# Four layers of attention and convolution on one core: scores of one image beside the output of the other, item 0 by chunks, out blocks in banks 6 and 7, and another filling of the last item

## What is computed

```
x = x + L0(_gn(x))   # lambda layer: q, k, v, softmax over positions, relative table
x = x + L1(_gn(x))   # 16 heads of 64, causal: 8 look back, 8 ahead; output projection Wo
x = x + L2(_gn(x))   # 16 heads of 64, attention with relative positions per head
x = x + L3(_gn(x))   # 3x3 convolution, tensor-train channel product, bias, relu
```

## Time and profile before

| | us |
|---|---|
| median of 3 runs (1408.1 to 1410.59) | 1408.25 |
| profiled execution, its own time | 1407.82 |
| its span | 1406.0 |
| PE busy (96% of the span) | 1348.8 |
| POOL busy (45%) | 627.2 |
| DVE busy (43%) | 608.4 |
| ACT busy (31%) | 436.7 |
| granted TensorE clock, mean | 0.987 |

### The profile page before, as it was taken

The page is one execution under the profiler, slowest core; times in us unless marked ns, Lnnn a source line. Parts: engine busy times, 40 slices in busy tenths (PEclk is TensorE's granted clock), DMA queues, the critical chain, the costliest instruction groups (busy, mean ns, idle before and its releaser), DMA issues.

```text
span 1406.0 us, 20610 instructions
## 1 busy us (share of the span) xinstructions
PE 1348.8 (96%) x7792; PEld 1057.7 (75%) x7792; DVE 608.4 (43%) x1385; ACT 436.7 (31%) x1053; POOL 627.2 (45%) x715
## 2 busy tenths in 40 slices
PE   4899889799999999999999999999999999999998
PEld 3688755457777787777788788788877887877887
DVE  6423422683454324445332445444144654356222
ACT  2220112022434311344330244534114444333222
POOL 2332279025454565545447443443654644445000
PEclk9999989999999999999999999999999999999999
DMA  5111035012222233222223221121322221210011
GB/s 192 38 46 45 30 61 92 0 40 71 67 74 69 68 84 85 72 68 68 69 68 98 67 62 53 61 66 56 85 81 60 61 61 54 68 54 23 1 54 66
DMA packets 57122, 89.23 MB, mean 63 GB/s; under 512 B 6880, under 2 KB 19840, under 8 KB 57024
## 3 DMA queue, kind: packets, MB, share of 16 engines
q1 hardware_dynamic: 55024, 84.59, 21.1%
q10 hardware_dynamic: 2000, 3.32, 0.7%
HBM read 79.50 MB, written 4.19 MB: 60 GB/s over the span
## 4 chain that ended last, share of the span: by engine, by line
PE 83%; DVE 2%; ACT 1%; issue 0%; POOL 0%; ACTq 0%; DVEq 0%; POOLq 0%
PE PS L1016 51%; PE PS L1493 6%; PE PS L1072 4%; PE PS L1090 3%; PE PS L856 3%; PE PS L1104 2%; PE PS L1060 2%; PE PS L862 2%; PE PS L1114 2%; PE PS L1133 2%; PE PS L1510 2%; DVE part L840 1%; PE PS L874 1%; PE PS L1081 1%; PE PS L1065 1%
## 5 line engine op out<-in xcount | busy, mean ns | idle before, releaser
L1016 PE MATMUL PS<-XB,w_hi 128*128 128x512 f32 x1024 | 359.4, 408 | 3.4 <-DVE XB L390 3.4
L210 POOL CAST w_hi<-w_raw 128x512 fp32r<-128x512 f32 x195 | 122.2, 627 | 402.5 <-PE PS L1016 294.3
L212 POOL TENSOR_TENSOR w_lo<-w_raw,w_hi 128x512 fp32r<-128x512 f32 x195 | 256.2, 1314 | 15.6
L1016 PEld LDWEIGHTS PS<-XB,w_hi 128*128 128x128 f32 x1024 | 192.7, 188 | 53.0 <-issue 7.2
L1016 PE MATMUL PS<-XB,w_lo 128*128 128x512 f32 x512 | 202.4, 395 | 0.0
L1016 PE MATMUL PS<-XB,part 128*128 128x512 f32 x768 | 200.2, 405 | 0.0
L1213 ACT ACTIVATE part<-PS,nmax 128x256 f32<-128x256 f32 (+1 forms) x256 | 111.5, 459 | 170.7 <-DVE nmax L1306 106.9
L1016 PEld LDWEIGHTS PS<-XB,part 128*128 128x128 f32 x768 | 140.8, 189 | 31.4
L210 POOL CAST part<-part 128x512 fp32r<-128x512 f32 x85 | 52.6, 619 | 150.9 <-PE PS L1016 150.9
L212 POOL TENSOR_TENSOR part<-part,part 128x512 fp32r<-128x512 f32 x85 | 110.7, 1302 | 6.8
L1016 PE MATMUL PS<-part,w_hi 128*128 128x512 f32 x344 | 112.2, 393 | 1.1 <-DVE part L1359 1.1
(11 more groups left out here) (142 smaller groups left out, 2033.6 us busy)
## 6 DMA issues: line engine op xcount, KB each, us to landing
w_raw<-in_w SPq DMA_DIRECT2D x187, 256.0 KB, 2.6
part<-in_w SPq DMA_DIRECT2D x85, 256.0 KB, 2.6
part<-part SPq DMA_DIRECT2D x32, 128.0 KB, 4.3
out_x<-xT SPq DMA_DIRECT2D x16, 256.0 KB, 2.1
xT<-in_x ACTq DMA_DIRECT2D x8, 256.0 KB, 8.2
xT<-in_x SPq DMA_DIRECT2D x8, 256.0 KB, 10.9
w_raw<-in_w SPq DMA_DIRECT2D x16, 128.0 KB, 3.8
part<-in_emb ACTq DMA_DIRECT2D x1, 961.0 KB, 13.0
```

The lines of the kernel that those rows point to most:

```text
L210: pool.tensor_copy(hi, raw).then_inc(w_hi_done, 1)
L212: pool.tensor_tensor(lo, raw, hi.bitcast(F32), ALU.subtract).then_inc(w_ready, 1)
L1016: m = nc.tensor.matmul(PS[:, bank, :], wt[:, (c % 4) * P:(c % 4) * P + P], rhs(hl, c), start=c == k == 0, stop=c == CK - 1 and k == 2)
```

## The change

Six edits. **Order on PE in an item**: `attend(i - 1, 1)` moves from the end of item i - 1 to just ahead of `scores(i, 0)`, and `scores(i, 1)` stands just behind `attend(i, 0)`; K and V are cut at other chunks. At a stage's end, attend of image 1 stays in its item, between chunks 3 and 4 of the next V. ACT and DVE follow: `evac_o` and `rest_of_o` move into the next item, `evac_t(i, 0)` ahead of `evac_q`, `evac_k` ahead of `evac_t(i, 1)`. **Out blocks** of stages 0 to 2 go to banks 6 and 7, and the wait for the sums moves from scores to `turn_values` and `attend(i, 0)`. **Item 0**: Q, K and V take turns by chunk over chunks 0 to 3, with V in bank 4, and the half-blocks are loaded in that order. **The last item**: chunks 4 to 7 of V of item 31 stand behind its scores 0, and out blocks 0 and 1 are cut more finely. **Factor products** stand in out blocks 2 to 7 alone, two in the middle and one at the end, where before there were two in each of eight. **Names**: `first_slot[key]` becomes `slots[key, half]`.

```
-        take_item(0)
+        take_item(0, (0,))
+        take_item(0, (1,))
...
+    def bank_of(i, kind):
+        return PT if (i, kind) == (0, "V") else PJ[kind]
     def out_bank(s, o):
-        return (0 if s == 3 else S) + o % 2
+        return (0 if s == 3 else O) + o % 2
...
         def scores(i, a):
-                if i % PAIRS == 0 and i:
-                    pe.wait_ge(sum_done, CK * (i // PAIRS))
         def turn_values(i):
             pe.wait_ge(v_evac, i + 1)
+            if i % PAIRS == 0 and i:
+                pe.wait_ge(sum_done, CK * (i // PAIRS))
         def attend(i, a):
+                if i % PAIRS == 0 and i:
+                    pe.wait_ge(sum_done, CK * (i // PAIRS))
         def out_block(s, o, chunks):
+                if c == 0 and o == 1 and s in (1, 2):
+                    pe.wait_ge(relh_evac, PAIRS * (s - 1) + 1)
+                    pe.wait_ge(relw_evac, PAIRS * (s - 1) + 1)
...
-        for kind in "QKV":
-            project(0, kind, range(CK))
-        for i in range(ITEMS):
-            final = i == ITEMS - 1
-            scores(i, 0)
-            project(i + 1, "Q", range(0, 4))
-            turn_values(i)
-            project(i + 1, "Q", range(4, CK))
-            scores(i, 1)
-            turn_probs(i, 0)
-            project(i + 1, "K", range(0, 2))
-            attend(i, 0)
-            relative(i + 1)
-            project(i + 1, "K", range(2, 6))
-            turn_probs(i, 1)
-            project(i + 1, "K", range(6, CK))
-            attend(i, 1)
-            project(i + 1, "V", range(CK))
...
+        for c in range(4):
+            for kind in "QKV":
+                project(0, kind, range(c, c + 1))
+        for kind in "QKV":
+            project(0, kind, range(4, CK))
+        for i in range(ITEMS - 1):
+            stage_ends = i % PAIRS == PAIRS - 1
+            if i % PAIRS:
+                attend(i - 1, 1)
+            scores(i, 0)
+            project(i + 1, "Q", range(0, 4))
+            turn_values(i)
+            project(i + 1, "Q", range(4, CK))
+            turn_probs(i, 0)
+            project(i + 1, "K", range(0, 3))
+            attend(i, 0)
+            scores(i, 1)
+            relative(i + 1)
+            project(i + 1, "K", range(3, CK))
+            project(i + 1, "V", range(0, 2))
+            turn_probs(i, 1)
+            if stage_ends:
+                project(i + 1, "V", range(2, 4))
+                attend(i, 1)
+                project(i + 1, "V", range(4, CK))
+                for o in range(CK):
+                    out_block(i // PAIRS, o, range(CK))
+            else:
+                project(i + 1, "V", range(2, 4 if i == ITEMS - 2 else CK))
+        i = ITEMS - 1
+        attend(i - 1, 1)
+        scores(i, 0)
+        project(i, "V", range(4, CK))
+        scores(i, 1)
+        out_block(3, 0, range(0, 3))
+        turn_values(i)
+        turn_probs(i, 0)
+        out_block(3, 0, range(3, 6))
+        attend(i, 0)
+        out_block(3, 0, range(6, 7))
+        out_block(3, 1, range(0, 2))
+        turn_probs(i, 1)
+        out_block(3, 1, range(2, 4))
+        attend(i, 1)
+        out_block(3, 1, range(4, 7))
+        for o in range(2):
+            out_block(3, o, range(7, CK))
+        for o in range(2, CK):
+            out_block(3, o, range(0, 4))
+            for k in range(2):
+                build_m(3 * (o - 2) + k)
+            out_block(3, o, range(4, CK))
+            build_m(3 * (o - 2) + 2)
...
     def attention_act(act):
             evac_v(i)
+            if i % PAIRS:
+                evac_o(i - 1)
             exps(i, 0)
+            evac_t(i, 0)
             evac_q(i + 1)
-            evac_t(i, 0)
             exps(i, 1)
             evac_relative(i + 1)
+            evac_k(i + 1)
             evac_t(i, 1)
-            evac_k(i + 1)
-            evac_o(i)
+            if i % PAIRS == PAIRS - 1:
+                evac_o(i)
...
     def attention_dve(dve):
             maxima(i, 0)
+            if j:
+                rest_of_o(i - 1)
             normalize(i, 0)
...
-            rest_of_o(i)
+            if j == PAIRS - 1:
+                rest_of_o(i)
```

More of the change, by code:

```diff
@@ L159, in build, with take, take_item @@
         sources = [None] * CK + list(range(CK, HB0))
[L160 to L166, removed]
+        slots = {}
+        def take(key, layer, kind, number, halves=range(2)):
+            for half in halves:
+                slots[key, half] = len(sources)
+                sources.append(block_at[layer, kind, number, half])
+        def take_item(i, halves=range(2)):
             for kind in "QKV":
-                take((i, kind), STAGES[i // PAIRS][0], kind, i % PAIRS)
-        take_item(0)
+                take((i, kind), STAGES[i // PAIRS][0], kind, i % PAIRS, halves)
+        take_item(0, (0,))
+        take_item(0, (1,))
         for i in range(ITEMS):
@@ L683, in later_layers @@
     w_load, w_split, w_slot, w_wait_used = (g[x] for x in ("w_load", "w_split", "w_slot", "w_wait_used"))
-    w_used, w_ready, slot_of, first_slot = (g[x] for x in ("w_used", "w_ready", "slot_of", "first_slot"))
+    w_used, w_ready, slot_of, slots = (g[x] for x in ("w_used", "w_ready", "slot_of", "slots"))
     w_raw, w_hi, sources = (g[x] for x in ("w_raw", "w_hi", "sources"))
@@ L1000, in later_layers, with chunk_of @@
     LO_KEYS = 2 * PAIRS
+    def bank_of(i, kind):
+        return PT if (i, kind) == (0, "V") else PJ[kind]
     def out_bank(s, o):
-        return (0 if s == 3 else S) + o % 2
+        return (0 if s == 3 else O) + o % 2
     def product_done(eng, key):
-        w_wait_used(eng, first_slot[key] + 1)
+        w_wait_used(eng, slots[key, 1])
     def attention_pe(pe):
-        def chunk_of(n, c, rhs, bank):
-            n += c // 4
+        def chunk_of(key, c, rhs, bank):
+            n = slots[key, c // 4]
             _, hi, lo = w_slot(n)
@@ L1201, in evac_v @@
             if layer_of(i) == 1:
-                ins = nc.scalar.activation(vT, PS[:, PJ["V"], :], ACT.Copy)
+                ins = nc.scalar.activation(vT, PS[:, bank_of(i, "V"), :], ACT.Copy)
             else:
@@ L1400, in attention_dve @@
                 for o in range(CK):
-                    if s == 3:
-                        rest_of_m(dve, 2 * o)
+                    if s == 3 and o >= 2:
+                        rest_of_m(dve, 3 * (o - 2))
+                        rest_of_m(dve, 3 * (o - 2) + 1)
                     add_out(s, o)
@@ L1405, in attention_dve @@
                         stats_of(s, o - 1)
-                    if s == 3:
-                        rest_of_m(dve, 2 * o + 1)
+                    if s == 3 and o >= 2:
+                        rest_of_m(dve, 3 * (o - 2) + 2)
                 stats_of(s, CK - 1)
@@ L1413, in attention_sp @@
             w_load(sp, n)
-            if n == first_slot[1, "Q"]:
+            if n == slots[(1, "Q"), 0]:
                 product_done(sp, (0, "Q"))
@@ L1436, in attention_pool @@
             for k in (2, 3):
-                if n == first_slot[3, "O", 0] + 4 * k:
+                if n == slots[(3, "O", 0), 0] + 4 * k:
                     masked_factor(pool, k)
@@ L1463, in rest_of_m @@
     def rest_of_m(dve, i):
+        if i >= 16:
+            return
         dve.wait_ge(m_hi, i + 1)
```

35 lines of the change are left out of this document (11 added, 24 removed).

## The result

The change made the kernel **slower**: 1415.49 us (median of 6 runs, 1414.26 to 1417.31) against 1408.37 us for the kernel before beside it, a ratio of 1.0054, 95% interval 1.0043 to 1.0065. The prediction said 1399.8 us and gave slower a chance of 0.05.

What follows compares the result with a forecast made beforehand. PE was taken as the bound, busy 1348.8 of 1406.0 us. Terms -3.0 - 4.6 - 4.7 + 4.35 - 0.6 = -8.5 us took 1407.8 to 1399.3, and 0.4 for the median gave 1399.8 us; range 1393.5 to 1405.0.

Steps and rivals of the forecast that it cites:

- Do the ordinary items get a new wait?: Ordinary items of layers 1 and 2: no new wait, 0 us; tightest are layer 1's second probability transposes, slack 1.0 us.
- rival D: Layer 1's 16 items: second probability transposes wait, making the kernel slower; example 1.0 us each, 1415.8 us; chance 0.06.
- Stage starts: At the three stage starts, the 1.0 us waits of scores for the last out-block sum go: -3.0 us.
- Item 0: Projections of item 0: chunk waits go, a 0.8 us weight-split wait comes, scores begin earlier: -4.6 us, bounds -3 to -5.5.
- Rival E: Item 0: the changed order gives nothing beyond half, since weight slots, not chunks, set its pace; 1402 us; chance 0.07.
- Switches in layer 1: Attend directly ahead of scores saves 2.9 us over 14 cross-item pairs, 1.8 over 16 inside items: -4.7 us.
- Rival B: Layer 1: no saving, attend into scores costs what both ways cost before; 1404.5 us; chance 0.11.
- Switches in layer 2: Scores between attend 0 and the relative products add 0.29 us in each of 15 items: +4.35 us, bounds 0 and +6.
- Rival A: Layer 2: scores between attend and the relative products cost nothing; 1395.4 us; chance 0.18.
- Last item: Item 31 to layer 3: old waits and lost clock go, new waits and one clock loss come: -0.6 us, bounds -3 and +3.
- three forecast waits: Item 31: scores 1 for exponentials 3.3 us, block 2 for a weight slot 1.5; layer 3 for the last sum 1.0.
- Rival C: Last item: worse, with the clock at 1.2 GHz for longer behind the 3.3 us wait; +3 us, 1403 us; chance 0.10.

Runs made afterwards that it cites:

- experiment 5: Kernel before with only out blocks of stages 0 to 2 in banks 6 and 7 and the sums' waits behind scores 0: 1404.07 us, ratio 0.9976.
- experiment 4: Kernel before with only the item 0 edit (Q, K, V by chunk over chunks 0 to 3, V in bank 4, half-blocks in that order): 1402.48 us, ratio 0.9963.
- experiment 6: Kernel before with only the new order of PE, ACT and DVE in layer 1's items 0 to 15: 1404.02 us, ratio 0.9973.
- experiment 1: Changed kernel, but in layer 2 ACT's copy of q waits for the relative products of the item before, not both scores: 1400.76 us, ratio 0.9953.
- experiment 2: Changed kernel, but in layer 2 scores 1 stand ahead of the first probability transposes, as before: 1396.50 us, ratio 0.9925.
- experiment 7: Kernel before, but in layer 2 scores 1 stand behind attend 0 and ACT copies transposed probabilities ahead of q: 1424.55 us, ratio 1.0123.

## Why the prediction was wrong

**The step that failed** is the paragraph "Do the ordinary items get a new wait?", which took 0 us. It went through probability transposes, V, the values' transposes, keys, attend and weight splits. Of the relative products it said only "Layer 2 has the relative products besides", as cover for others. But they read q too, and had got a new neighbour without being moved. The step ahead had put scores 1 directly before them and priced three switches there, 0.29 us, without asking what the relative products wait for. The wait is not in the order that PE's rows show; it is in `evac_q`, where ACT waits for both scores of the item. It cost 16 x 0.84 = 13.4 us by the list of waits, some 14.7 us by the stretches (16 x 0.92). The last sentence of the prediction named the sign ("Any wait that repeats per item would make me wrong"), but rival D had it in layer 1, at the probability transposes, and priced the chance of any such wait by that one place. Its example, 1.0 us of wait in each of 16 items and 1415.8 us, comes within 0.4 us of the measured time by coincidence: in layer 1 the probability transposes have no wait at all.

**Stage starts**: -3.0 forecast, -3.5 measured (experiment 5). **Item 0**: -4.6 forecast, -4.1 measured (experiment 4); the split's wait was 1.0 and not 0.8 us, and the 72 products took 17.5 instead of 17.2. Rival E fell. **Switches in layer 1**: -4.7 forecast, -4.8 measured without item 15's wait (experiment 6); an item of 22.7 us. Rival B fell. Scores directly behind attend start 0.84 us after it (338.72 to 339.56), as a 512-column product does (360.06 to 360.90 before); what is paid once less is the 0.11 us of the first product behind attend and the 0.10 us of the way from a product into scores. How the 4.8 us divide between the pairs across items and those inside one was not taken apart:

```profile
338.72 0.91 PE L1122 MATMUL PS<-part,part 128*64 128x128 f32 x16
339.56 0.95 PE L1064 MATMUL PS<-part,part 64*128 64x128 f32 x12
```

The Trainium skill, TensorEngine Tiling (Array Packing), Key Properties, says that changing the tiling mode drains TensorE. Attend (128*64) and scores (64*128) are of two modes by the shapes in these rows, and the trace shows no extra time between them: the scores take 1.09 us behind attend, and 1.09 or 1.12 behind a product of V or Q before. So the page's rule does not give the price here; the rows do.

**Switches in layer 2**: +4.35 forecast, 4.4 to 4.5 measured (experiments 1 and 2), and none once scores 1 stand elsewhere (experiment 2). Rival A fell. **Last item**: -0.6 forecast, +0.6 measured with layer 3, the terms that were mis-sized. All three forecast waits came out within 0.2 us, and the clock stayed at full speed behind layer 3's wait, as forecast. Two gains were counted whole that were worth half. The 1.7 us of lost clock in the old last item were worth 0.85 only (last section): where the clock was not lowered, PE reached its wait earlier and stood longer. And of the 1.5 us of clock won in layer 3, 0.7 went into a new wait: the chain shows PE's products of that stretch released by DVE's chunk, which PE now reaches before it is normalised:

```profile
1318.84 0.61 DVE XB L1612
1319.45 0.04 issue
1319.50 5.58 PE PS L1534 x23
```

-0.6 + 0.85 + 0.7 is +0.95, within 0.4 of what was measured; that rest is open. Nor is +0.6 itself a firm number, as it sets one execution beside one. In the five executions with the old end (before and experiments 4 to 7) last item and layer 3 take 178.8 to 180.6 us together, 179.7 on average, and the profile of before is the longest of them. In the three with the changed end (the changed kernel, experiments 1 and 2) they take 181.2 on average without the 12 products of V. By these the term is +1.5. Rival C had the right sign, but not its reason: the clock behind the new wait lost 1.7 us, about the 1.5 in the sum, and not more.

So the sum of the terms it had was right to about 2 us: with the one wait taken away (experiment 1) the kernel is 6.6 us faster than before by the ratio, 4.6 to 8.7 by the interval, where -8.5 was forecast. That the profiled spans are 8.3 us apart (1406.0 and 1397.7) is closer partly by luck: the errors of stage starts and item 0 cancel, 0.4 us lie ahead of item 0, and the profile of before had a long end. The error that turned the sign is the missing term.

## What to carry over

When a piece is moved directly ahead of another, ask of the one behind it what it reads, who makes that on another engine, and what that engine waits for, down to the conditions that protect a buffer: such a condition may name the very piece that has been moved in. A condition that is wider than it needs to be (here both scores, where the copy's buffer has one reader) may cost nothing until the order changes, as this one did. And a list of "tightest" waits is safe only if it goes through every piece behind the moved one, small ones too.

## What the hardware did that was not expected

The same instructions, behind the same waits, got a different clock from one execution to the next, at three places. What decides it is open. The first is the old last item, which the kernels of before and of experiments 4 to 7 share (experiments 5 to 7 ran on one chip). 16 us after the start of scores 0 of item 31, in before and in experiment 4 (columns as in the earlier trace rows):

```profile
1241.43:1249.43 8.00, 5.78 (x27) 3.89 (x24) 3.30 (x4) 4.51 (x6) 2.15 (x3) 0.79 0.00 0
```

```profile
1236.83:1244.83 8.00, 5.10 (x30) 3.34 (x29) 4.07 (x5) 4.62 (x6) 2.75 (x4) 1.00 0.00 0
```

At a mean of 0.79 (part of it at 1.2 GHz, the rest at 2.4) the way from scores 0 to layer 3 takes 62.84 us, and 62.82 in experiment 5; at 1.00 it takes 62.01, and 61.98 and 61.96 in experiments 6 and 7. 8 x 0.21 = 1.7 us of clock cost 0.85 us of time. The rows show where much of the other half went. Before, then experiment 4:

```profile
1246.86 1.05 PE L1155 MATMUL PS<-ttA,part 96*128 96x256 f32 x4
1249.75 0.50 PE L1155 MATMUL PS<-ttA,part 96*128 96x256 f32 x2 [0.72 <-DVE part L1466]
```

```profile
1241.62 0.98 PE L1161 MATMUL PS<-ttA,part 96*128 96x256 f32 x4
1244.31 0.51 PE L1161 MATMUL PS<-ttA,part 96*128 96x256 f32 x2 [1.00 <-DVE part L1475]
```

The wait for a split factor product shrank from 1.00 to 0.72 us, and the four factor products ahead of it took 0.85 us at a granted clock of 0.50 (1246.86 to 1247.71) and 0.82 at 1.00 (1241.62 to 1242.44). In a stretch that waits for other engines, a slow clock uses up part of the idle time.

The second is item 0. Experiment 6 leaves it as it was, and the wait ahead of the last chunk is 0.86 us as before, but the 12 products behind it take 4.96 instead of 3.46 us (308.86 to 313.82, against 308.58 to 312.04). Experiment 6:

```profile
305.00:312.00 7.00, 5.49 (x14) 4.12 (x15) 6.23 (x18) 1.44 (x3) 1.89 (x2) 0.63 0.27 72
```

Before it was 0.76 there, and item 0 lasted 22.69 against 24.20 us. The changed kernel, with other waits (one of 1.04 us in that stretch), stayed at full clock:

```profile
305.00:312.00 7.00, 5.96 (x26) 4.55 (x25) 6.37 (x24) 1.09 (x2) 5.82 (x7) 1.00 0.12 37
```

The third is the start of layer 3, behind the 2.2 us wait. The first 8 us of layer 3 in before and in experiment 5:

```profile
1288.27:1296.27 8.00, 8.00 (x28) 6.39 (x29) 5.97 (x31) 2.46 (x5) 4.36 (x8) 0.79 0.01 2
```

```profile
1284.20:1292.20 8.00, 8.00 (x35) 6.52 (x36) 5.96 (x31) 2.48 (x5) 4.34 (x8) 1.00 0.01 2
```

It was 0.79 in experiments 4 and 6 too, and 1.00 in experiment 7. So the prediction's gain of 1.5 us there is one that the old kernel had in two of five executions without any change.

So part of what a removed wait gives back is clock, and one profiled execution doesn't tell its size: it differs by 0.85 us in the last item, by 1.5 us in item 0 and by about 1 us in layer 3 (its first 192 products take 46.1 to 46.4 us at the lower clock, 45.0 and 45.2 at the full one) between executions of equal code.
